# Small triangular products alternating between array strips, a preamble whose gate rows lie as the units read them, and a unit's order of work written anew

## The reference, cut to what matters

```python
x = x + _layernorm(attn(_layernorm(x), W_qkv, W_z, W_b, W_a, W_out, conv_w, dt_bias, A_log, norm_w))
x = x + _layernorm(ffn(_layernorm(x), lut, gate_idx, up_idx, down_idx))

# attn: mixed = silu(causal_conv4(x @ W_qkv.T));  q, k, v = split(mixed);  q, k = l2norm(q), l2norm(k)
beta = sigmoid(x @ W_b.T);  g = -exp(A_log) * softplus(x @ W_a.T + dt_bias);  gc = cumsum(g in a chunk)
A = -(k_beta @ k.T * decay) * strict          # decay[i, j] = exp(gc_i - gc_j), lower triangle
Tm = inv(eye - A)                             # unit lower triangular
u, kcd = Tm @ v_beta, Tm @ (k_beta * exp(gc))
# scan over the chunks, state S:
v_new = u - kcd @ S;  out = (q * exp(gc)) @ S + (q @ k.T * decay) @ v_new
S = S * exp(g_last) + (k * exp(g_last - gc)).T @ v_new
# then out * rsqrt(mean(out^2)) * norm_w * silu(x @ W_z.T) @ W_out.T, summed over the heads
```

## Time and profile before

| | us |
|---|---|
| median of 3 runs | 4870.68 (4868.75 to 4873.02) |
| profiled execution, its own time | 4866.2 |
| its span in the trace | 4864.0 |
| PE busy | 4643.0 (95%) |
| DVE, ACT, POOL busy | 3760.0, 2864.6, 2725.4 |
| granted TensorE clock, mean | 0.98 |

### The profile page before, as it was taken

The page is one execution under the profiler, slowest core; times in us unless marked ns, Lnnn a source line. Parts: engine busy times, 40 slices in busy tenths (PEclk is TensorE's granted clock), DMA queues, the critical chain, the costliest instruction groups (busy, mean ns, idle before and its releaser), DMA issues. The chain is left out here.

```text
span 4864.0 us, 98703 instructions
## 1 busy us (share of the span) xinstructions
PE 4643.0 (95%) x33236; PEld 3450.4 (71%) x33236; DVE 3760.0 (77%) x8539; ACT 2864.6 (59%) x5549; POOL 2725.4 (56%) x8582
## 2 busy tenths in 40 slices
PE   4699999999999999999999999999999999998697
PEld 2377777777777777777777777777777777776344
DVE  4588888888888888888888888888888888885564
ACT  2366666666666666666666666666666666663111
POOL 0366666666666666666666666666666666664000
PEclk8799999999999999999999999999999999999899
DMA  4111112212122111122121221221221112210200
GB/s 132 38 42 38 44 40 46 47 42 46 39 53 47 37 44 42 43 54 47 33 55 38 45 47 36 45 49 44 46 54 34 44 40 45 47 32 18 100 14 18
DMA packets 579249, 219.43 MB, mean 45 GB/s; under 512 B 455212, under 2 KB 541612, under 8 KB 577080
## 3 DMA queue, kind: packets, MB, share of 16 engines
q1 hardware_dynamic: 578744, 213.13, 18.5%
HBM read 161.02 MB, written 52.00 MB: 44 GB/s over the span
## 5 line engine op out<-in xcount | busy, mean ns | idle before, releaser
L718 DVE SCALAR_TENSOR_TENSOR CV<-pp,CW,CV 128x1023 f32<-128x1023 f32 (+2 forms) x768 | 980.6, 1277 | 115.0 <-ACT CV L1002 108.0
L428 PE MATMUL pp<-xnT,W 128*128 128x512 f32 x2048 | 977.1, 601 | 40.6 <-DMA W<-wqkv 30.8
L1222 POOL TENSOR_TENSOR TM<-UL,XL 128x126 f32<-128x126 f32 (+22 forms) x1984 | 701.7, 354 | 277.8 <-issue 140.5
L1225 POOL TENSOR_TENSOR UL<-UL,TM 128x126 f32<-128x126 f32 (+22 forms) x1984 | 734.5, 370 | 155.4
L428 PEld LDWEIGHTS pp<-xnT,W 128*128 128x128 f32 x2048 | 375.9, 194 | 313.4 <-issue 268.3
L1086 ACT ACTIVATE QE<-qa,TAB 128x128 f32<-128x128 f32 x1024 | 319.8, 364 | 457.5 <-PE qa L553 455.8
L595 PE MATMUL emit<-Wz,xnT 128*128 128x256 f32 x2048 | 505.1, 389 | 1.0 <-DVE OACC L892 1.0
L616 PE MATMUL emit<-Wo,NTr 128*128 128x256 f32 x2048 | 497.8, 386 | 3.1 <-ACT NTr L1131 1.4
L1283 POOL TENSOR_TENSOR wd<-wd,wv 128x268 f32<-128x268 f32 x240 | 224.3, 934 | 475.3 <-DVE wv L903 475.3
L1097 ACT ACTIVATE VS<-qa,EB 128x128 f32<-128x128 f32 x1024 | 320.2, 366 | 234.6 <-PE qa L563 225.9
L827 DVE SCALAR_TENSOR_TENSOR R<-kv,TAB,V 128x128 f32<-128x128 f32 x1024 | 310.1, 344 | 182.4 <-PE kv L543 177.8
(11 more groups left out here) (197 smaller groups left out, 9667.2 us busy)
## 6 DMA issues: line engine op xcount, KB each, us to landing
W<-wqkv SPq DMA_DIRECT2D x256, 128.0 KB, 2.9
XL<-xb SPq DMA_DIRECT2D x128, 256.0 KB, 3.9
UL<-c_u SPq DMA_DIRECT2D x64, 256.0 KB, 2.9
xb<-X SPq DMA_DIRECT2D x512, 32.0 KB, 1.6
Wz<-wz SPq DMA_DIRECT2D x64, 256.0 KB, 3.4
ub<-UL SPq DMA_DIRECT2D x128, 128.0 KB, 3.0
N<-ub SPq DMA_DIRECT2D x256, 64.0 KB, 2.2
Wo<-wo SPq DMA_DIRECT2D x64, 256.0 KB, 3.1
```

Source lines behind the costliest of these rows:

```text
L428: ins = t.matmul(bk.pp[:, 512 * h:512 * h + 512], m.W[:, c, k, :], m.xnT[:, w // KH % 2, c, 512 * h:512 * h + 512], start=c == 0, stop=c == 1)
L718: v.scalar_tensor_tensor(m.CV[:, t, d:S], bk.pp[:, 0:S - d], m.CW[:, w % KH, t, 3 - d:4 - d], m.CV[:, t, d:S], ALU.mult, ALU.add).then_inc ...
L1222: p.tensor_tensor(m.TM[:, 0:a, 0:b], m.UL[:, 0:a, k:k + 1].to_broadcast([128, a, b]), m.XL[:, k, k + 1:32].unsqueeze(1).to_broadcast([128, ...
L1225: p.tensor_tensor(m.UL[:, 0:a, k + 1:32], m.UL[:, 0:a, k + 1:32], m.TM[:, 0:a, 0:b], ALU.subtract).then_inc(s["sub"], 1)
```

## The change

Four things change.

1. In `m1` the left and right products alternate, and in `m2` the three kinds do. The copies behind them now wait for the whole block. Both kinds of `y1` must be there before `m2` begins.
2. The preamble is no stage of its own. Each engine has a `start()` (preamble and first steps of unit 0, in buffers of the loop that are still free), then one barrier, then `loop()`, which begins with `tables()`. `wb` has no zeros any more: gate products are 32 columns wide and each sequence's rows go to its own 32 partitions. The first 8 tiles of x are normalized first, with a `newton` of their own. Part of the stores to DRAM move to POOL's queue; the tables' buffers are `XL`, `Wz`, `Wo` and `V[0]`, so `xl`, `ldz`, `ldo`, `ldt` and the first `vev` wait for the tables' stores.
3. The order of calls in an iteration is new on all five engines; an iteration now begins behind `m2(u, 0)` and `ks(u-1, 7)`.
4. `newton` has 3 rounds in place of 4.

```diff
-    for i in range(4):
+    for i in range(3):
...
         for u in range(8):
-            ins = t.matmul(bk.ml[32:64, u * 32:(u + 1) * 32], m.X[w % 2][0:32, 8 * h + u, 32:64], m.VL[0:32, 8 * h + u, 0:32],
-                           start=True, stop=True)
-        ins.then_inc(s["m1"], 1)
-        for u in range(8):
-            ins = t.matmul(bk.mr[96:128, u * 32:(u + 1) * 32], m.X[w % 2][64:96, 8 * h + u, 96:128], m.VL[64:96, 8 * h + u, 0:32],
-                           start=True, stop=True)
-        ins.then_inc(s["m1"], 1)
+            left = t.matmul(bk.ml[32:64, u * 32:(u + 1) * 32], m.X[w % 2][0:32, 8 * h + u, 32:64], m.VL[0:32, 8 * h + u, 0:32],
+                            start=True, stop=True)
+            right = t.matmul(bk.mr[96:128, u * 32:(u + 1) * 32], m.X[w % 2][64:96, 8 * h + u, 96:128],
+                             m.VL[64:96, 8 * h + u, 0:32], start=True, stop=True)
+        left.then_inc(s["m1"], 1)
+        right.then_inc(s["m1"], 1)
...
+        rows = (bk.ml, bk.mr, bk.kv, bk.qa)
+        for part in range(2):
+            for half in range(2):
+                for b in range(NB):
+                    for h in range(2):
+                        ins = t.matmul(rows[2 * part + half][32 * b:32 * b + 32, :], p.wb[:, h, part, :],
+                                       p.xnT[b][:, h, 512 * half:512 * half + 512], start=h == 0, stop=h == 1)
+                ins.then_inc(s["rowp"], 1)
...
+    def start():
+        po.wait_ge(s["xtp"], NT // 2)
+        gp.memset(m.N1[0][:], 0.0)
+        gp.memset(m.N1[1][:], 0.0)
+        nk(0)
+        for k, d in enumerate((dr.gcd, dr.gad)):
+            po.wait_ge(s["pieces"], 5 * k + 5)
+            for b in range(1, NB):
+                gp.dma_start(d[:, :, b * S:b * S + S], p.pieces[k][32 * b:32 * b + 32]).then_inc(s["g3w"], 16)
```

More of the change, by code:

```diff
@@ L308, in ldg @@
         kh, t0 = w % KH, w // KH * S
+        if w == 0:
+            sp.wait_ge(s["g3a"], 32)
+        else:
+            sp.wait_ge(s["g3w"], 96)
         sp.wait_ge(s["decp"], 4 * w)
@@ new lines, in loop @@
+    def loop():
+        ldx(0)
+        ldx(1)
+        index(0)
+        ldx(2)
+        ldw(1, 0)
+        ldw(1, 1)
+        ldw(1, 2)
+        index(1)
+        xo(0, 0)
+        xo(0, 1)
+        decoded(0)
+        xl(0)
+        ui(0)
+        ldt(0)
+        ldg(1)
+        uo(0)
+        ldo(0)
+        nl(0)
+        ldw(1, 3)
+        ldx(3)
+        ldw(2, 0)
+        ldw(2, 1)
+        ldw(2, 2)
+        for u in range(NU + 2):
+            index(u + 2)
+            xo(u + 1, 0)
+            xo(u + 1, 1)
+            decoded(u + 1)
+            xl(u + 1)
+            ui(u + 1)
+            ldz(u)
+            ldt(u + 1)
+            ldg(u + 2)
+            uo(u + 1)
+            ldo(u + 1)
+            nl(u + 1)
+            ldw(u + 2, 3)
+            ldx(u + 4)
+            ldw(u + 3, 0)
+            ldw(u + 3, 1)
+            sto(u - 2)
+            ldw(u + 3, 2)
+        sp.wait_ge(s["dwd"], 16 * KH)
+        sp.wait_ge(s["doa"], 16 * NB)
@@ L418, in main_pe @@
+    return start, loop
+def main_pe(nc, s, g, m, p, bk):
     pe, t = Engine(nc.tensor), nc.tensor
@@ new lines, in tables @@
+    def tables():
+        banks = (bk.out, bk.ml, bk.mr, bk.kv)
+        for k, (row, ready) in enumerate(((p.ra, "gst"), (p.rb, "bst"))):
+            pe.wait_ge(s[ready], 5 if k == 0 else 3)
+            pe.wait_ge(s["rows"], 4)
+            for h in range(2):
+                pb = banks[2 * k + h]
+                for n in range(4):
+                    c = 4 * h + n
+                    ins = t.transpose(pb[:, n * 128:(n + 1) * 128], row[:, c * 128:(c + 1) * 128], g.ident)
+                ins.then_inc(s["colp"], 1)
+        pe.wait_ge(s["l127"], 16)
+        pe.wait_ge(s["col"], 2)
+        for h, pb in enumerate((bk.qa, bk.out)):
+            t.matmul(pb[:, :], p.last127, p.GC[:, 16 * h:16 * h + 16, :], start=True, stop=True).then_inc(s["glp"], 1)
@@ L708, in main_dve @@
+    return start, loop
+def main_dve(nc, s, g, m, p, bk):
     dv, v = Engine(nc.vector), nc.vector
@@ L987, in main_act @@
+    return start, loop
+def main_act(nc, s, g, m, p, bk):
     ac, a = Engine(nc.scalar), nc.scalar
@@ new lines, in program @@
+            w = m.NTr[:].rearrange("p u d -> p (u d)")
+            p.mv = w[:, 0:2 * NT].rearrange("p (n k) -> p n k", k=2)
+            p.var, p.rstd, p.tn, p.hd = (w[:, 128 + 32 * i:160 + 32 * i] for i in range(4))
+            p.wb = m.DEC[0][:, 0, :].rearrange("p (h k n) -> p h k n", h=2, k=2)
+            parts = (main_sp(nc, s, g, m, p, dr), main_pe(nc, s, g, m, p, bk), main_dve(nc, s, g, m, p, bk),
+                     main_act(nc, s, g, m, p, bk), main_pool(nc, s, g, m, p, dr))
+            for start, loop in parts:
+                start()
@@ L1666, in program @@
+            nc.all_engine_barrier()
+            for start, loop in parts:
+                loop()
             nc.all_engine_barrier()
```

1217 lines of the change are left out of this document (672 added, 545 removed).

## The result

The changed kernel takes 4779.02 us (median of 4 runs, 4778.30 to 4784.59), the kernel before 4871.23 us on the same chip: a ratio of 0.981, 95% interval 0.980 to 0.982. The forecast was 4715. The kernel is faster, as forecast; the gain is 92 us instead of 151 to 156. The two profiled executions differ by less, 81.5 us, since the one before (4866.2 us) lies 5.0 us under that median and the one after (4784.6 us) 5.6 us over its own; what follows splits these 81.5.

The account below looks back on a forecast made before the run. In the units PE's own sequence was taken as the bound, ahead of them a chain over several engines. From 4866.2: -105 units, -42 preamble, -4 newton gave 4715 us; own range 4685 to 4750, wide range 4660 to 4785.

Parts of the forecast that it names:

- the 66.3: Sign of being wrong: units staying over 66.3 us; forecast unit 65.3 us, bounds 64.7 to 66.3.
- The joins: m1 and m2 on PE: alternating calls save 0.40 us in each of 4 blocks, 1.6 us a unit.
- The page's rule: Skill page's sequencer bound, about 62 ns a matmul: m1 never under 0.99 us; prediction kept its row, used this as rival.
- The order's waits: PE's waits under the new order: 1.2 us a unit where there were 1.4, -0.2; bounds 0.6 and 2.2.
- tenths elsewhere: Small unlisted waits in a unit, added to the walked ones to reach 1.2 us.
- the strip's slow place: vn and tpk on PE, where tpk waits for the strip and sup for copies behind vn: 0.6 us a unit, unchanged.
- My walk: New lists walked with the trace's distances: PE waits about 0.1 at ks(1), 0.1 at ks(5), 0.2 to 0.3 us at ks(7).
- A new wait of 1 us a unit: Rival: new wait at the end of DVE's list or behind POOL's solve, +63, 4778 us; chance 0.15.
- joins which gain little: Rival: m1 at 43 ns a call, m2 unchanged, 0.66 us a unit, 4774; or nothing, 4816; chance 0.10, of it 0.04 nothing.
- The preamble: Before the first ks: gate products on four column places and x(0,3) earlier, -42 us; bounds -28 and -52.
- Newton and the end: Feed-forward stage: a round less per newton, three exposed, -2.4, as much again where PE waits for DVE: -4 us.

## Why the prediction was right, and where its size was wrong

The side was right, and 4779 lies inside the wide range (4660 to 4785). It lies outside the forecast's own (4685 to 4750), and a unit of 66.40 us is over the 66.3 that the prediction itself named as a sign of being wrong. So the time fell into the range on a mechanism that was wrong in one step.

**The joins** (1.6 us a unit, "any microsecond taken from PE's own sequence counts, unless another engine becomes late"): the blocks' lengths were right to 0.01 us. That they count was right only for the order they came with. Undone in it, a unit grows by 1.18 us (67.58 - 66.40), three quarters of 1.59: chunks 0 and 1 give their 0.40 in full (7.48 to 7.08, 9.12 to 8.72), chunk 6 gives 0.56 of 0.80 (9.47 to 8.91), and chunk 7 takes 0.13 back. In the old order they count for nothing. One can split the change the other way too: the new order with the old joins costs 0.62 us a unit (67.58 - 66.96), where the forecast had 0, and the joins then bring 1.18 instead of 1.6. Either way it is the waits that were misjudged.

**The page's rule.** The Trainium skill, "TensorE: Matmul & The Clock Gate", section "Wait — 56ns, not 53.3ns?", gives about 62 ns of sequencer time a matmul as a bound for the case that hardware decode is off. The prediction left that condition out, and no run here shows the setting. As the prediction took it, the bound is not borne out: m1's 16 calls take 0.62 us, 39 ns each, and m2's 24 take 0.64 us, 27 ns each.

**The order's waits** ("with tenths elsewhere I get 1.2 us of waits where there were 1.4"): this is the step that failed. With 84 blocks at their unhindered distance (63.4 - 1.59), 12 visits of 0.19 and a period of 66.31 (start to start over 57 units), 2.2 us of waits are left, 1.0 more than forecast. 1.0 x 63 = 63 us is most of the 70 by which the profiled execution misses (4784.6 against 4715). By place, each block's distance less its unhindered one and less 0.09 or 0.10 at a mode's edge: the strip's slow place 0.86 (I had 0.6), ks(7) 0.23, ks(1) and ks(3) 0.18 each, m3(u,0) 0.15, sup(0) and ks(6) 0.12 each, ks(5) 0.11, z(u-1,3) 0.08, m4(u,1) 0.06, rest 0.05. My walk had ks(1), ks(5) and ks(7), about right. The rest of the list, with what the slow place takes over 0.6, makes 1.0 us, and for that my "tenths elsewhere" were 0.1 to 0.2. The slow place was misread, not changed: counted over all of its blocks it took 0.82 us before too. Two things were left out of the walk. A semaphore that comes late costs its lateness and about 0.10 us beside: ks(1), ks(3) and ks(6) take 0.54 us to the next block, where ks(2) with its state in time takes 0.43. In PE's timeline of the kernel after, sup(0), at(0), ctp, ks(1) and qs(1), then ks(2) and qs(2):

```profile
1980.96 0.70 PE L468 MATMUL kv<-VS,K 128*128 128x256 f32 x2
1981.49 0.61 PE L478 MATMUL qa<-VN,AT 128*128 128x128 f32 x4
1981.94 0.60 PE L501 MATMUL emit<-cf,CO 128*128 128x128 f32 x4
1982.45 0.70 PE L439 MATMUL kv<-St,QK 128*128 128x256 f32 x2
1982.99 0.59 PE L449 MATMUL qa<-St,QK 128*128 128x256 f32 x2
...
1991.17 0.59 PE L439 MATMUL kv<-St,QK 128*128 128x256 f32 x2
1991.60 0.59 PE L449 MATMUL qa<-St,QK 128*128 128x256 f32 x2
```

No row shows idle time, yet ctp takes 0.51 us to ks(1) where it needs 0.44, and ks(1) takes 0.54 where ks(2) takes 0.43. And I walked PE and VectorE but neither ScalarE's list, on which m3(u,0) waits (u12r behind dec), nor sup(2) to ks(3) and sup(5) to ks(6). The distance sup to ks is 1.39 to 1.50 us in five of eight chunks, where before only two were under 2 us (1.56 and 1.89).

**The last unit.** Some 5 us more of the miss lie outside of the steady period, and no term of the forecast had them. After the change the first distance between clearings is 68.2 us, 1.8 over the steady 66.3, and the last is 69.7 us (4295.5 to 4365.2), 3.4 over it. Before, the last was 61.8 us (4378.6 to 4440.4), under the steady 67.0. The ends of these two last stretches, first after, then before (columns as in the earlier trace rows):

```profile
4360.00:4365.20 5.20, 5.20 (x31) 4.29 (x30) 2.13 (x6) 1.13 (x2) 0.00 (x0) 0.73 0.00 0
```

```profile
4430.00:4440.40 10.40, 9.86 (x80) 7.85 (x76) 4.89 (x16) 4.13 (x10) 2.12 (x5) 1.00 0.01 2
```

In the new order PE had stood idle for 3.06 us ahead of ctp at 4355.2, and the clock granted behind that was 0.59 from 4355 to 4360 and 0.73 up to the clearing, and op took 3.4 us to the next block instead of 1.8. Before, the granted clock was 1.00 there.

**The rivals.** A new wait of 1 us a unit gave 4778, which is nearly what was measured, but that is luck. In the steady units m1 follows its block without waiting for VL, so POOL's solve is in time, and of the end of DVE's list only ks(7)'s 0.23 us came. The waits lie at ten places, most of them small. That joins which gain little gave 4774 is luck too: both were as short as forecast.

**The preamble** (-42): -39.5. Its parts: the last gate product near 45 (51 forecast), the barrier at 84 (90), x(0,3) at 118.8 (122), the first ks at 183.0 (183). The 3 us gained ahead of x(0,3) went again on the way from x(0,3) to m1, 50.8 us instead of 47.8; from m1 to the first ks it is 13.4 us instead of 16.3, as forecast. **Newton and the end** (-4): -6.3. No run has the preamble or the shorter newton alone, so how these two parts come about is read from the trace and not tested.

## What to carry to other kernels

Where several engines work one list each and meet at fixed points (here each ks), the period is better read as a sum of maxima than as one engine's busy time: between two meetings counts the longest list, or the latency of the loop that they meet for (here 1.39 to 1.50 us from sup to ks). A shorter block pays only where its own engine's list is the longest. Ask for busy time by window between the meeting points; a share over the whole unit hides a stretch in which the second engine is full to 98%. So judge a faster operation and the order around it together (here nothing clear of the noise alone, 79 us in the new order), and expect a wait that is removed to reappear in part at the next full list: of nine kernels here that moved or cut single calls one gained some 10 us, four changed nothing clear of the noise, and four lost.

## What the runs showed of the hardware that was not expected

Products on different 32-column strips of the array run beside each other for long ones too. The gate products (128x512, 128 rows by 32 columns) were issued to four strips in turn, two products to each. Their rows in PE's timeline of the kernel after, from inside that stretch:

```profile
40.15 0.63 PE L544 MATMUL mr<-xnT,DEC 128*32 128x512 f32 x2
40.22 0.61 PE L544 MATMUL mr<-OACC,DEC 128*32 128x512 f32 x2
40.58 0.63 PE L544 MATMUL mr<-xnT,DEC 128*32 128x512 f32 x2
```

A product has two records here as elsewhere. Two rows of two records start 0.07 us apart and the next two 0.43 us later, so four records take 0.43 us, as long as one record at full width; two of the four read xnT and two OACC, which fits one on each strip. The 64 records of the 32 products run from 38.0 to 45.1 us, where the 64 of full width took 36.1 to 63.8; the granted clock was 1.00 in both stretches. I had allowed 12 us for what took 7. POOL's issue of a DMA costs 0.56 to 0.73 us each for the gate rows and 1.15 to 1.20 us for the tables. At the barrier behind the gate rows POOL's queue drains for 4.8 us, to 83.5, which is what the barrier at 84 waits for.
